# The 16-wide attention layer: q and k projected in nine output tiles of 128 columns in place of twelve of 96, and q's turned copy made by GpSimd

## What is computed

```
xn = layer_norm(x)                        # 1024 tokens, 192 channels
q, k, v = xn @ wq + bq, xn @ wk + bk, xn @ wv + bv      # 12 heads of width 48 = 576 columns each
logits = q k^T / sqrt(48) + q . Rh[row_q - row_k] + q . Rw[col_q - col_k]    # 256 x 256 per image and head
x2 = x + softmax(logits) @ v @ wo + bo
x3 = x2 + gelu(layer_norm(x2) @ w1 + b1) @ w2 + b2
```

## Time and profile before

| | |
|---|---|
| median of 3 runs | 608.25 us (605.36 to 612.27) |
| the profiled execution | 613.67 us, of which the span of instructions is 611.9 us |
| mean granted TensorE clock | 0.952 |
| PE busy | 540.6 us, 88% |
| DVE busy | 294.9 us, 48% |
| ACT busy | 230.0 us, 38% |
| POOL busy | 127.7 us, 21% |

### The profile page before, as it was taken

One profiled execution on the slowest core, in us unless ns is written; L12 is line 12 of the kernel. 1 busy time (PEld: TensorE's weight loads), 2 busy tenths in 40 slices (PEclk: granted clock), 3 DMA queues, 4 the chain that ended last, 5 costly groups with the idle time before them and its releaser, 6 DMA issues.

```text
span 611.9 us, 10105 instructions
## 1 busy us (share of the span) xinstructions
PE 540.6 (88%) x3864; PEld 384.2 (63%) x3864; DVE 294.9 (48%) x776; ACT 230.0 (38%) x453; POOL 127.7 (21%) x194
## 2 busy tenths in 40 slices
PE   7968999899989858898998999989878897999997
PEld 5726767674754344554655686575457675848676
DVE  4734867663134251456547543054648676611143
ACT  4303544525334214364464324423145455351110
POOL 8003000103004232251643204311030001120020
PEclk9977997999999967899999899997989999999999
DMA  6893467003313435636356402800734540020001
GB/s 167 197 186 70 95 123 251 1 2 100 90 55 93 97 79 112 156 74 151 88 130 161 136 1 60 186 21 22 158 82 108 111 134 2 2 66 1 0 1 51
DMA packets 21863, 55.39 MB, mean 91 GB/s; under 512 B 4560, under 2 KB 10248, under 8 KB 21688
## 3 DMA queue, kind: packets, MB, share of 16 engines
q1 hardware_dynamic: 21432, 54.65, 37.1%
q0 software_dynamic: 384, 0.10, 0.1%
HBM read 12.28 MB, written 0.79 MB: 21 GB/s over the span
## 4 chain that ended last, share of the span: by engine, by line
PE 63%; DVE 16%; SPq 9%; DMA 5%; ACT 4%; issue 4%; DVEq 0%; ACTq 0%
PE PS L1219 60%; DVE NM L1115 5%; DMA QA<-REL 3%; DVE REL L1100 3%; SPq L732 2%; PE PS L1235 2%; SPq L724 2%; SPq L742 2%; ACT REL L944 1%; DMA PT<-in_qm 1%; DVE HL L1125 1%; SPq L680 1%; ACT OT L923 1%; DVE OT L1147 1%; SPq L681 1%
## 5 line engine op out<-in xcount | busy, mean ns | idle before, releaser
L1115 DVE TENSOR_REDUCE NM<-PS 98x2 f32<-98x392 f32 (+2 forms) x192 | 105.6, 569 | 94.0 <-PE PS L1219 92.6
L964 ACT ACTIVATE PT<-PS 98x392 f32<-98x392 f32 (+2 forms) x192 | 95.0, 519 | 73.9 <-PE PS L1219 72.4
L1219 PE MATMUL PS<-KA,QA 128*98 128x196 f32 (+3 forms) x432 | 91.9, 310 | 28.3 <-DVE NM L1115 23.0
L1219 PEld LDWEIGHTS PS<-KA,QA 128*98 128x98 f32 (+3 forms) x432 | 64.8, 190 | 56.1 <-DVE NM L1115 30.8
L1219 PE MATMUL PS<-QA,KA 128*98 128x196 f32 (+2 forms) x480 | 91.1, 291 | 6.2 <-ACT PT L964 1.8
L1219 PEld LDWEIGHTS PS<-QA,KA 128*98 128x98 f32 (+2 forms) x480 | 70.0, 185 | 21.3 <-issue 11.2
L1219 PE MATMUL PS<-XT,WQKV 128*96 128x512 f32 (+1 forms) x128 | 56.7, 697 | 12.1 <-ACT OT L923 7.4
L1219 PE MATMUL PS<-NR,SEL 128*98 128x392 f32 x144 | 52.1, 362 | 0.6 <-DVE NR L1137 0.6
L1219 PE MATMUL PS<-XT,W 128*128 128x512 f32 (+1 forms) x144 | 51.6, 614 | 0.0
L1219 PE MATMUL PS<-PT,V 128*32 128x196 f32 (+2 forms) x672 | 50.6, 345 | 0.0
L1100 DVE TENSOR_TENSOR REL<-PS,REL 32x512 fp32r<-32x512 f32 (+5 forms) x64 | 28.5, 480 | 44.3 <-ACT REL L944 43.9
(11 more groups left out here) (107 smaller groups left out, 698.9 us busy)
## 6 DMA issues: line engine op xcount, KB each, us to landing
QA<-QHL SPq DMA_DIRECT2D x36, 192.0 KB
KA<-KHL SPq DMA_DIRECT2D x24, 228.0 KB
QA<-REL SPq DMA_DIRECT2D x24, 224.0 KB
QA<-QHL SPq DMA_DIRECT2D x12, 384.0 KB
KA<-KHL SPq DMA_DIRECT2D x12, 384.0 KB
KA<-PT SPq DMA_DIRECT2D x12, 380.0 KB
QA<-REL SPq DMA_DIRECT2D x24, 128.0 KB
W<-in_w SPq DMA_DIRECT2D x3, 768.0 KB, 4.4
```

The lines of the kernel that those rows point to most:

```text
L964: nc.scalar.activation(dst, src, ACT.Exp).then_inc(probs_done.sem, 1)
L1115: nc.vector.tensor_reduce(dst, src, AX.X, ALU.max, negate=True).then_inc(max_done.sem, 1)
L1219: return nc.tensor.matmul(dst, lhsT, rhs, start=start, stop=stop, skip_group_check=loose)
```

## The change

In layer 1 alone, q and k of two neighbouring chunks (c even, c+1) are computed in three tiles of 128 output columns: the 96 rows of q of chunk c with rows 64 to 95 of its k; the same for chunk c+1; and rows 0 to 63 of k of both chunks. The weights are packed on the host in this order. The `k` steps of odd chunks issue nothing on TensorE and ScalarE. ScalarE evicts from a q tile the 32 rows of k and the 96 rows of q, and from a k tile 64 rows to the second chunk's k and 64 rows to the first's. The odd chunks' k lies in a new buffer `k2`, which is group 4 of OT. ScalarE no longer writes the turned copy QX: GpSimd copies it from QD, one copy for each token half, before it splits q, and `rh`/`rw` on TensorE wait for these copies (`q_turned`). Before it writes a later q tile ScalarE also waits for the k split of two chunks before. The `inverse` of group 4 waits for the last k split.

```
+def qk_tile(L, step, c):
+    if L.pads:
+        return c + (L.chunks if step == "k" else 0)
+    return c // 2 * 3 + (2 if step == "k" else c % 2)
 ...
+            m["k2"] = m["OT"][0:CK, L.groups - 2, :]
 ... GpSimd
+                if step == "q":
+                    if i:
+                        pool.wait_ge(*psum_of["rw"].at(n, 2 * (i - 1) + 1))
+                    for w in range(2):
+                        part = slice(2 * w, 2 * w + 2)
+                        turned = m["QX"].rearrange("r (b x y) -> r b y x", b=NB, x=IMG)
+                        pool.wait_ge(*q_done.at(n, 2 * i + w))
+                        nc.gpsimd.tensor_copy(turned[:, part], image(m["q"])[:, part])\
+                            .then_inc(q_turned.sem, 1)
                 if i:
                     for wait in chunk_read(L, i - 1):
                         pool.wait_ge(*wait)
                 pool.wait_ge(*done.at(n, 2 * i + 1))
-                nc.gpsimd.tensor_copy(part[:, 0, :], m[step]).then_inc(hi_done.sem, 1)
+                src = m["k2"] if step == "k" and i % 2 and not L.pads else m[step]
+                nc.gpsimd.tensor_copy(half[:, 0, :], src).then_inc(hi_done.sem, 1)
 ... ScalarE, layer 1
+                    if step == "q":
+                        if i:
+                            act.wait_ge(*psum_of["rw"].at(n, 2 * (i - 1) + 1))
+                            act.wait_ge(*q_lo.at(n, i - 1))
+                        else:
+                            act.wait_ge(*skb_done.at(n, 0))
+                        if i >= 2:
+                            act.wait_ge(*k_lo.at(n, i - 2))
+                    elif i % 2:
+                        continue
+                    elif i:
+                        act.wait_ge(*k_lo.at(n, i - 1))
+                    for w in range(2):
+                        act.wait_ge(*psum_of[step].at(n, 2 * i // (1 + (step == "k")) + w))
+                        src, tokens = PS[:, unit_bank[step, w], :], slice(w * 512, (w + 1) * 512)
+                        if step == "k":
+                            pieces = ((m["k2"][0:64, tokens], slice(64, 128)), (m["k"][0:64, tokens], slice(0, 64)))
+                        else:
+                            pieces = ((m["k2" if i % 2 else "k"][64:CK, tokens], slice(CK, 128)),)
+                        for dst, p in pieces:
+                            ins = nc.scalar.activation(dst, src[p], ACT.Identity, bias=SKB[n][p, tile:tile + 1],
+                                                       scale=L.scale)
+                        if step == "k" or i % 2:
+                            ins.then_inc(k_done.sem, 1)
+                        if step == "k":
+                            continue
+                        bias = COL[n][0:CK, 8 + tile:9 + tile]
+                        nc.scalar.activation(m["q"][:, tokens], src[0:CK], ACT.Identity, bias=bias)\
+                            .then_inc(q_done.sem, 1)
+                    continue
-                        if not L.pads:
-
-                            turned = m["QX"].rearrange("r (b x y) -> r b y x", b=NB, x=IMG)[:, 2 * w:2 * w + 2]
-                            ins = nc.scalar.activation(turned, src.rearrange("r (b y x) -> r b y x", b=2, y=IMG),
-                                                       ACT.Identity, bias=bias)
 ... TensorE
+                if part and c % 2 and not L.pads:
+                    continue
-                mm(PS[0:CK, bank, :], WQKV[:, 1 - u, cols], tokens[u][1 - u], True, False)
+                mm(PS[0:size, bank, :], WQKV[:, 1 - u, cols], tokens[u][1 - u], True, False)
-                    pe.wait_ge(*q_done.at(n, 2 * c + 1))
+                    pe.wait_ge(*(q_done if L.pads else q_turned).at(n, 2 * c + 1))
```

More of the change, by code:

```diff
@@ L65, in __init__ @@
         self.slot = 32 if head_dim == 16 else 64
+        self.qk_tile, self.qk_tiles = (CK, 2 * self.chunks) if head_dim == 16 else (128, 3 * self.chunks // 2)
+        self.column = 8 + self.qk_tiles
         self.vcol = 32 if head_dim == 16 else 50
@@ L437, in _build @@
     WQKV = sb(ctx, "WQKV", [128, 2, 3 * max(L.dim for L in LAYERS)])
-    COL = [sb(ctx, f"COL{L.index}", [128, 8 + 2 * L.chunks + FM]) for L in LAYERS]
-    SKB = [sb(ctx, f"SKB{L.index}", [CK, L.chunks]) for L in LAYERS]
+    COL = [sb(ctx, f"COL{L.index}", [128, L.column + FM]) for L in LAYERS]
+    SKB = [sb(ctx, f"SKB{L.index}", [L.qk_tile, L.qk_tiles]) for L in LAYERS]
     VB = [sb(ctx, f"VB{L.index}", [128, L.dim]) for L in LAYERS]
@@ L534, in _build @@
     two = per(lambda L: 2 * L.chunks)
-    psum_of = {kind: count(kind + "_psum", two) for kind in ("q", "k", "rh", "rw")}
+    psum_of = {kind: count(kind + "_psum", two) for kind in ("q", "rh", "rw")}
+    psum_of["k"] = count("k_psum", per(lambda L: 2 * L.chunks if L.pads else L.chunks))
     q_done, k_done = count("q_done", two), count("k_done", two)
+    q_turned = count("q_turned", per(lambda L: 0 if L.pads else 2 * L.chunks))
     rh_done, rw_done = count("rh_done", two), count("rw_done", two)
@@ L817, in _ @@
             if step in ("q", "k") and u == 1 and not (L.pads and (step == "q" or i == 0)):
-                part, done, hi_done, lo_done = (m["QHL"], q_done, q_hi, q_lo) if step == "q" else \
+                half, done, hi_done, lo_done = (m["QHL"], q_done, q_hi, q_lo) if step == "q" else \
                     (m["KHL"], k_done, k_hi, k_lo)
+                if step == "q":
[7 more added lines that the diff above has]
+                            .then_inc(q_turned.sem, 1)
                 if i:
@@ L826, in _ @@
                     pool.wait_ge(*pad_keys.at(n, i))
-                nc.gpsimd.tensor_copy(part[:, 0, :], m[step]).then_inc(hi_done.sem, 1)
+                src = m["k2"] if step == "k" and i % 2 and not L.pads else m[step]
+                nc.gpsimd.tensor_copy(half[:, 0, :], src).then_inc(hi_done.sem, 1)
                 pool.wait_ge(*hi_done.at(n, i))
                 if L.pads:
-                    nc.gpsimd.tensor_copy(part[:, 1, :], part[:, 0, :].bitcast(F32))
-                nc.gpsimd.tensor_tensor(part[:, 2 if L.pads else 1, :], m[step], part[:, 0, :].bitcast(F32),
+                    nc.gpsimd.tensor_copy(half[:, 1, :], half[:, 0, :].bitcast(F32))
+                nc.gpsimd.tensor_tensor(half[:, 2 if L.pads else 1, :], src, half[:, 0, :].bitcast(F32),
                                         ALU.subtract).then_inc(lo_done.sem, 1)
@@ L907, in _ @@
                     continue
+                tile = qk_tile(L, step, i)
+                if not L.pads:
+                    if step == "q":
[28 more added lines that the diff above has]
+                    continue
                 if i:
@@ L1138, in _ @@
             elif step == "inverse":
-                if i + u == 0 and L.pads:
+                if (i + u == 0) if L.pads else (i == L.groups - 2 and u == 0):
                     dve.wait_ge(*k_lo.at(n, L.chunks - 1))
@@ L1272, in _ @@
                 unit_bank[step, u] = bank
-                cols = slice(part * D + c * CK, part * D + (c + 1) * CK)
+                size, tile = L.qk_tile, qk_tile(L, step, c)
+                cols = slice(tile * size, (tile + 1) * size)
                 tokens = [[permuted(m, k, w) if permute else XT[:, k, w * 512:(w + 1) * 512] for k in range(2)]
                           for w in range(2)]
-                mm(PS[0:CK, bank, :], WQKV[:, 1 - u, cols], tokens[u][1 - u], True, False)
+                mm(PS[0:size, bank, :], WQKV[:, 1 - u, cols], tokens[u][1 - u], True, False)
                 if u:
@@ L1546, in _pack @@
         order = np.arange(2 * L.dim).reshape(2 * L.chunks, L.per_chunk, L.hd).transpose(0, 2, 1).ravel()
+        if not L.pads:
+            q, k = order.reshape(2, L.chunks, CK)
+            order = np.concatenate([rows for c in range(0, L.chunks, 2) for rows in
+                                    (q[c], k[c, 64:], q[c + 1], k[c + 1, 64:], k[c, :64], k[c + 1, :64])])
         order = np.concatenate([order, np.arange(2 * L.dim, 3 * L.dim)])
         wqkv, bqkv = wqkv[:, order], bqkv[order]
-        col = np.zeros((128, 8 + 2 * L.chunks + FM), np.float32)
+        col = np.zeros((128, L.column + FM), np.float32)
         at = 0
-        for c in (*map(deep, (g1, o1, g2, o2)), cols(bqkv[:2 * L.dim], CK), cols(b1, 128)):
+        for c in (*map(deep, (g1, o1, g2, o2)), cols(bqkv[:2 * L.dim], L.qk_tile), cols(b1, 128)):
             col[:len(c), at:at + c.shape[1]] = c
```

22 lines of the change are left out of this document (10 added, 12 removed).

## The result

| | before | after |
|---|---|---|
| median, 20 runs each | 612.44 us | 606.10 us |
| lowest to highest | 605.36 to 616.86 | 601.2 to 614.76 |
| profiled execution, and its span | 613.67, 611.9 | 607.03, 605.2 |
| mean granted clock in it | 0.952 | 0.952 |
| PE busy | 540.6 us | 530.5 us |

The ratio is **0.9933, 95% interval 0.9904 to 0.9961**. Run again with its text unchanged beside other kernels, the changed kernel gave 609.94 us against 611.25, ratio 1.0004 [0.9954, 1.0054]. Ratios leave out disturbed runs, so they can differ a little from the quotient of two medians.

A forecast was written before the change was run, and what follows sets the result against it. Bound: PE's own order in head pairs; waits among PE, VectorE and ScalarE around chunk 1. Terms +0.3 - 3.5 - 1.7 - 1.3 - 0.3 = -6.5 us, scaled to 601.8 us; own range 598 to 605, wider range 596 to 608.

The forecast's parts named there:

- chunk 1: Layer 1, chunk 1: its k and wait vanish, but GpSimd holds VectorE's second rounding: -3.5 us, or -5.1 if not held.
- the start: Start of layer 1: rh waits for GpSimd's second copy and the V tiles queue behind: +0.3 us (-0.1 to +0.6).
- chunks 3 and 5: Odd chunks: PE saves 2.99 us each, but the maxima row's DMA caps the gain: -1.7 and -1.3 us.
- The anchor: Whole kernel: profiled gain scaled to the 608.25 us median, 608.25 x 607.2 / 613.67 = 601.8 us.
- the copy: GpSimd's two added turned copies of 96 x 512 per chunk: 1.02 us each, 0.61 to 1.28 us as bounds.
- ScalarE's spacing: ScalarE's q evictions: straight ones every 0.59 us, four in 2.36 us, so exponentials come 0.59 us sooner.
- chunks 2 and 4: Even chunks: k starts up to 0.6 us sooner, two more evictions hold banks: -0.3 us together, bounds -1.2 and +1.2.
- A: Rival: PE's time comes back whole, rows land in time and the rounding is not held: -12.4 us, 596 us; chance 0.28.
- H: Follow-up theory, odd chunks 3 and 5: GpSimd's longer stretch holds VectorE's two rounding instructions of the maxima.
- S: Follow-up theory, odd chunks 3 and 5: ScalarE's evictions stand ahead of its exponentials.
- B: Rival: GpSimd becomes the bound, a copy costing 2.04 us: -1.0 us, 607 us, no change; chance 0.20.
- C: Rival: TensorE's clock falls in the pairs of the odd chunks 3 and 5: +12.3 us, 620 us; chance 0.07.

The follow-up runs named there:

- the repeat: The changed kernel run again unaltered, in the profiled execution of its second measurement: median 609.94 us, ratio 1.0004 to the kernel before.
- e3: The changed kernel with GpSimd's copies written straight instead of turned, so rw reads q in the wrong order: 607.87 us, ratio 0.9985.
- e2: The kernel before, with its twelve tiles of 96, plus only the turned copy moved to GpSimd: 607.49 us, ratio 0.9971.
- f4: The changed kernel with GpSimd waiting for the rounding before divide, late eviction of odd chunks' 32 k rows, own banks for rh/rw in chunk 0: 604.37 us, ratio 0.9924.
- g1: f4 without GpSimd's wait ahead of divide: 606.93 us, ratio 0.9901.
- g2: f4 with GpSimd's wait ahead of divide only for groups 0 and 2, beside chunks 3 and 5: 604.44 us, ratio 0.9877.
- e4: The changed kernel with layer 1's divide cut from 512 to 8 columns, leaving most outputs of groups 0 to 4 undivided: 602.52 us, ratio 0.9881.
- f2: The changed kernel with GpSimd waiting, ahead of divide, until VectorE has rounded the next pair's maxima: 608.16 us, ratio 0.9954.
- g3: The changed kernel with GpSimd waiting in chunk 1 for head 1's rounding before it splits k: 607.00 us, ratio 0.984.

## Why the prediction was right or wrong

**The direction was right and the size was not.** Forecast: 6.5 us of 613.67. Measured: 4.3 us at equal clock, ratio 0.9933, which is within the 1% that I called no change. 606.1 us lies in the range, above the 601.8 forecast. The second measurement's interval, 0.9954 to 1.0054, does not exclude that nothing changed.

**Luck.** The two profiled executions lie 6.6 us apart and the two medians 6.3, close to the 6.5 of the forecast. The second measurement has 1.3 us between its medians. And the terms of the profiled execution were others than the forecast's: -6.0 us in chunk 1, from a case that the repeat did not have, and -2.7 in the two stages that go with the clock, against +2.2 at the start and only -1.3 in chunks 3 and 5.

**The anchor.** The forecast was scaled to 608.25 us, a median of three runs. Twenty runs of the same kernel give 612.44. That alone puts the forecast 4 us too low; the profiled execution, 613.67, was nearer to the usual run than the median of three.

**Right, to 0.1 us: the copy.** 1.02 forecast, 1.04 to 1.08 in its rows. The straight one came out at 609 ns, the lower end that I had from the casts, and turned over straight is 1.74 where ScalarE has 1.66. The Trainium skill's half as much again for a read step over 8 bytes (GPSIMD Engine Reference, Performance pitfalls for Q7 kernels) would have given an estimate of some 0.83 us; for these writes, the runs decide against carrying it over. e3 shows that the term hardly mattered for the whole: 0.36 us in chunk 3, nothing in the kernel's time.

**Mis-sized: ScalarE's spacing.** I had evictions every 0.59 us; four straight ones in a row start 0.70 us apart (208.60, 209.30, 210.01, 210.72 in chunk 1). So a q tile costs ScalarE 2.71 us, 0.24 less than before, not 0.59. The row that I took 0.59 from is a straight eviction with a turned one behind it.

**Missed: the bank at the start.** The forecast gave the start +0.3. It was +2.2: 0.7 from the first eviction to rh (4.08 against 3.36 us), 0.84 because rw's second unit waits for k's two further evictions, and 0.67 ahead of the first eviction, with the granted clock at 0.50 in 180 to 184 us where before it was 0.65, which is no doing of the forecast's terms (1.00 in e2). I had counted that cost of k's evictions in chunks 2 and 4 and not in chunk 0. Own banks took the 0.84 us away (f4, g1, g2: 1.91 us between rh and V).

**Right: chunk 1.** -3.5 us forecast with the rounding held, -3.6 in the repeat; the profiled execution had the unheld case, -6.0 against the -5.1 I gave for it. Which of the two comes is decided by less than a tenth of a microsecond: an instruction of VectorE that started 0.02 us ahead of GpSimd's TENSOR_TENSOR took 0.17 us (216.94 in the rows above), one that started 0.01 us behind it 2.35 (e3). The Trainium skill's rule (GPSIMD Engine Reference, Specifications), that GpSimd and VectorE share their SBUF interfaces, agrees with these rows, 0.17 against 1.87 us.

**The step that failed: chunks 3 and 5.** I wrote that PE saves 2.99 us and "can gain no more than these 2.0 us less 0.3", because of the DMA of the row of maxima. The two terms, -1.7 and -1.3 us, came out at -0.67 and -0.65, so 1.7 us of the forecast's sum were not there, and PE waits for no row at the scores of head 4 or 8. Only head 9's scores wait for theirs, 2.07 us, and before they waited 1.7. The row landed in 3.0 us, not 4.2; this is its line in the DMA view of 256 to 276 us, after:

```profile
QA<-NR POOLq DMA_DIRECT2D x1, 8.0 KB, 3.0
```

Two things stood there instead. One is the hold that I had priced in chunk 1 and forgotten here: PE's saved time moved the rounding from beside k's split, behind `divide`, to beside q's split and `divide`, which held it until `divide` ended (+1.65 us in chunk 3 of the profiled execution). `divide` ends 14.4 us after head 3's transpose, 0.5 later than before, and what follows it is 1.2 us shorter; that makes the 0.67. e4 took the hold away and gained 1.93. The other is ScalarE: the scores wait 1.93 us in place of k's 1.28. I had named that wait, but the 2.9 us that I counted leave it only 2.99 + 1.28 - 2.9 = 1.37 us.

**Chunks 2 and 4.** -0.3 for both; chunk 4 took 0.43 us more, in the direction of the upper bound: rh now waits 0.92 us for k's four evictions, and k's first unit only 0.31 us less than before. Chunk 2 can't be told from the clock.

**The rivals.** A (-12.4 us) failed by H and S; f4 and g2 show that even without both, the transfers behind k's split take the rest. B named GpSimd as the bound, by a copy at double price. The price was wrong, but the engine was right: the end of `divide` sets the stage of chunks 3 and 5, through VectorE's rounding, which it holds. C came in a mild form, right behind PE's wait for the exponentials: the clock is 1.00 beside chunk 3 after, but 0.57 in 308 to 312 us, beside chunk 5, and 0.66 and 0.63 in the two pairs of the repeat. It cost these stages nothing (15.90, 15.89 and 15.92 us), since `divide` ended later than PE's work. In f2, without the hold, it did (0.58 in 268 to 272 us).

**Open.** Why stretches at the lower clock fall where they do, which moves single runs by several us, was not tried, and with it whether the change itself costs clock. What the nine tiles add to the copy is not settled, nor is g3's worth.

## What to carry to other kernels

When matmuls are taken out of a busy pair, list what the other engines do at the moment at which PE will now arrive: here a 128 x 8 rounding moved under GpSimd's long instructions and a score met ScalarE's evictions, and 3 us of PE's work became 0.7. Price a neighbour effect that you have found once in every place where the two engines meet, not only where you found it. Time each half of a change alone: here one half was as quick as both. And when runs spread with the granted clock, compare kernels at equal clock before you believe a median of three, and look at the mean clocks too.

## What the hardware showed beside this

A VectorE instruction of 128 x 8 elements that starts while GpSimd works on SBUF takes what is left of GpSimd's instruction, or of the one right behind it: 0.17 us alone, 1.87 and 2.35 us beside a TENSOR_TENSOR of 96 x 1024, 0.33 us beside the end of a CAST. In layer 1 of the thirteen traces 106 roundings started beside a copy, cast or product of GpSimd, and each ended within 0.11 us of the end of a GpSimd instruction; the other 206 took 0.17 us. VectorE's reductions from PSUM kept their 0.65 to 0.69 us beside GpSimd's work as without it. ScalarE's eviction of 512 columns takes 0.68 us for 32, 64 and 96 partitions alike. A GpSimd copy that writes with a step of 64 bytes costs 1057 ns, the straight one 609.
